# A state scan in halves or whole: merging the two half-row decays and scans of a Mamba block

## The chip, the cores and the metric

One core of one Trainium2 chip. The metric is the device time of one execution in microseconds (us). Times are written as the profile has them: us from the start of the span, durations in us unless marked ns. The five engines are PE (TensorE), DVE (VectorE), ACT (ScalarE), POOL (GpSimd) and SP (SyncE); PEld is the loading of weights into PE.

## The reference

The input is `x` of 8 sequences x 512 positions x 128 features, all fp32. Four layers follow one another, each of the form x = x + f(layernorm(x)): a Mamba block, a feed-forward block with ternary weights, a minimal GRU, and the same feed-forward block again. The change touches the Mamba block, whose core is a linear recurrence over the 512 positions, for 256 inner channels and 16 states:

```python
dA = jnp.exp(dt_s[..., None] * A)
hstate = dA * hstate + (dt_s * u_s)[..., None] * B_s[:, None, :]
y = jnp.einsum('bdn,bn->bd', hstate, C_s)
```

`dt` and `u` depend on sequence, position and channel, `A` on channel and state, `B` and `C` on sequence, position and state. The state starts at zero for every sequence.

## The kernel before, in words

The 256 channels lie as two halves (`HALVES`) of 128 partitions; positions run along the free dimension. So for one sequence b and one state n the whole recurrence is two rows of 512 elements per partition. The kernel walks over the 8 sequences and, inside, the 16 states: 128 steps, numbered g = 16 b + n. One step is:

- `mix_decay` (ACT, lines 700 and 702): dA = exp(dt * A), one ACTIVATE per half, into the PSUM tensor `dA` of 2 x 512 elements. There is a single `dA`, so a decay overwrites what the scan of the step before has read.
- `mix_inflow` (POOL, line 381; the very first on DVE): `inflow` = dtu * B, both halves in one instruction, in two buffers. It waits until the scan of step g - 2 is done.
- `mix_scan` (DVE, lines 922 and 925): `tensor_tensor_scan`, state = dA * previous + inflow along the 512 positions, one instruction per half, into one of three `state` buffers.
- `mix_cn` (PE, line 1197): a matmul that spreads C over the partitions into the PSUM tensor `c_ps`; it waits for the read of the step before.
- `mix_read` (DVE, line 933): state = state * C, both halves in one instruction.
- `mix_acc` (PE, line 1206): eight 128x128 transposes that add the result to `y_ps`.

The halves are chained by their own semaphores: the decay of half 0 waits for the scan of half 0 of the step before (`s_scan0`), the decay of half 1 for that of half 1 (`s_scan`); the scan of half 0 waits for the decay of half 0 (`s_dA0`), that of half 1 for the decay of half 1 (`s_dA`).

Everything else, that is all four layers of the earlier and later sequences, is woven between these steps. Each operation has a due time in steps, from tables written out at the top (`POOL_AT`, `ACT_AT`, `DVE_AT`, `PE_AT`, with exceptions for the first and the last sequence in `MOVED`), and every engine emits its operations in the order of these times, in quarter steps. Each engine then runs its queue strictly in order and waits on semaphores. The decay of step g is due at g - 1, the scan at g, the read at g + 0.75. Between them stand on ACT the normalisations (`n_tok`, L716, `n_hi`, L723), GELU and its table loads (L735), the GRU's inputs (L748, L753) and gates (L766); on DVE the GRU's products and scans (L1018, L1024), `in_hi` (L1009), `n_lo` (L985), statistics (L955 to L964) and residual sums (L948, L1002, L1031); on POOL `in_lo` (L536), roots and sums. PE's other products share three PSUM banks, `work`, in an order fixed when the program is built. SP issues all DMAs.

Of the kernel before, what the change touches and what calls it, by code (L numbers as in the profile page):

```python
# [12 lines left out]
ALU = mybir.AluOpType  # L13
ACT = mybir.ActivationFunctionType
# [3 lines left out]
ROWS, SEQ, D = 8, 512, 128  # L18
# [3 lines left out]
STATE = 16  # L22
# [159 lines left out]
def build(nc, x, gamma, beta, W_in, W_conv, b_conv, W_x, W_dt, b_dt, A_log, Dskip, W_out,  # L182
          W1, b1, W2, b2, Wz, bz, Wh, bh, Wo, bo, w_up, w_down, out):
    ctx = ExitStack()
    with ctx:
        def sb(name, shape, dt=F32):
            return ctx.enter_context(nc.sbuf_tensor(name, shape, dt))

        def sem(name):
            return ctx.enter_context(nc.semaphore(name))  # L190

        def flat(a):
            return a.rearrange("p a b -> p (a b)")
# [3 lines left out]
        ones = sb("ones", [P, P])  # L197
# [9 lines left out]
        decay_c = sb("decay_c", [P, HALVES, STATE])  # L207
# [27 lines left out]
        dt = sb("dt", [P, 2, HALVES, SEQ])  # L235
# [3 lines left out]
        inflow = sb("inflow", [P, 2, HALVES, SEQ])  # L239
        state = sb("state", [P, 3, HALVES, SEQ])  # L240
# [11 lines left out]
        scale = {m: sb("scale%d" % m, [P, TILES]) for m in NORMS}  # L252
# [28 lines left out]
        def pb(name, shape):  # L281
            return ctx.enter_context(nc.psum_tensor(name, shape, F32))

        dA = pb("dA", [P, HALVES, SEQ])
# [22 lines left out]
        s_conv, s_u, s_ztok = sem("conv_added"), sem("u_ready"), sem("z_tok_ready")  # L307
        s_xdhi, s_brow = sem("xd_hi_ready"), sem("b_row_ready")
        s_sparg, s_spexp, s_spln = sem("softplus_args"), sem("softplus_exp"), sem("softplus_ln")
        s_dt, s_dtu = sem("dt_ready"), sem("dtu_ready")  # L310
        s_bstored, s_bring = sem("b_stored"), [sem("b_ring%d" % k) for k in range(RING)]
        s_y0, s_cps = sem("y_started"), sem("c_full")
        s_dA0, s_scan0 = sem("decay_half_ready"), sem("scan_half_done")
        s_dA, s_inflow, s_scan, s_read, s_acc = (sem("decay_ready"), sem("inflow_ready"), sem("scan_done"),
                                                 sem("read_ready"), sem("acc_done"))
        s_gtok = sem("gated_tok_ready")
# [13 lines left out]
        def wait(eng, s, value):  # L330

            if value > 0:
                eng.wait_ge(s, value)
# [258 lines left out]
        def _(act):  # L592
# [102 lines left out]
            def mix_decay(b, n):  # L695

                if n == 0:
                    act.wait_ge(s_dt, HALVES * b + HALVES)
                wait(act, s_scan0, STATE * b + n)
                act.activation(dA[:, 0, :], dt[:, b % 2, 0, :], ACT.Exp, scale=decay_c[:, 0, n:n + 1]).then_inc(s_dA0, 1)  # L700
                wait(act, s_scan, STATE * b + n)
                act.activation(dA[:, 1, :], dt[:, b % 2, 1, :], ACT.Exp, scale=decay_c[:, 1, n:n + 1]).then_inc(s_dA, 1)  # L702

            def mix_gated(b, h, r, s):
                p = "gt%d" % h
# [65 lines left out]
            for r, s in slots():  # L771
# [6 lines left out]
                for n in range(STATE):  # L778
                    for b in due(r, s, ACT_ON["decay"], n):
                        mix_decay(b, n)  # L780
# [46 lines left out]
        def _(dve):  # L827
            def prepare_mix():
                dve.wait_ge(s_w_mix, W_MIX)
                dve.tensor_copy(win_hi[:, :], win_f).then_inc(s_win_hi, 1)  # L830
                dve.tensor_copy(wdt_hi[:, :], wdt_f).then_inc(s_wdt_hi, 1)
                dve.wait_ge(s_win_hi, 1)
                dve.tensor_tensor(win_lo[:, :], win_f, win_hi[:, :].bitcast(F32), ALU.subtract).then_inc(s_win, 1)
                dve.wait_ge(s_wdt_hi, 1)
                dve.tensor_tensor(wdt_lo[:, :], wdt_f, wdt_hi[:, :].bitcast(F32), ALU.subtract).then_inc(s_wdt, 1)
                for h in range(HALVES):
                    last = dve.tensor_scalar(diag[:, h, :], ident[:, :], skip_c[:, h:h + 1], None, ALU.mult)
                last.then_inc(s_diag, 1)
                dve.wait_ge(s_expA, 1)
                dve.tensor_scalar(decay_c[:, :, :], decay_c[:, :, :], -1.0, None, ALU.mult).then_inc(s_A, 1)  # L840

            def ternary_sums():
                dve.wait_ge(s_w_tail, W_TAIL)
                dve.tensor_reduce(abs_sum[:, 0:1], up_raw, AX_X, ALU.add, apply_absolute_value=True
                                  ).then_inc(s_abs, 1)
                dve.tensor_reduce(abs_sum[:, 1:2], down_raw, AX_X, ALU.add, apply_absolute_value=True
                                  ).then_inc(s_abs, 1)
# [68 lines left out]

            def mix_scan(b, n):
                g = STATE * b + n
                dve.wait_ge(s_dA0, g + 1)
                dve.wait_ge(s_inflow, g + 1)  # L920
                wait(dve, s_acc, g - 2)
                dve.tensor_tensor_scan(state[:, g % 3, 0, :], dA[:, 0, :], inflow[:, n % 2, 0, :],  # L922
                                       0.0, ALU.mult, ALU.add).then_inc(s_scan0, 1)
                dve.wait_ge(s_dA, g + 1)
                dve.tensor_tensor_scan(state[:, g % 3, 1, :], dA[:, 1, :], inflow[:, n % 2, 1, :],  # L925
                                       0.0, ALU.mult, ALU.add).then_inc(s_scan, 1)

            def mix_read(b, n):
                g = STATE * b + n
                dve.wait_ge(s_scan0, g + 1)  # L930
                dve.wait_ge(s_scan, g + 1)
                dve.wait_ge(s_cps, g + 1)
                dve.tensor_tensor(state[:, g % 3, :, :], state[:, g % 3, :, :],  # L933
                                  c_ps[:, :].unsqueeze(1).broadcast_to([P, HALVES, SEQ]), ALU.mult
                                  ).then_inc(s_read, 1)
# [101 lines left out]
            for r, s in slots():  # L1037
# [8 lines left out]
                for n in range(STATE):  # L1046
                    for b in due(r, s, DVE_ON["scan"], n):
                        mix_scan(b, n)
                for n in range(STATE):
                    for b in due(r, s, DVE_ON["read"], n):  # L1050
                        mix_read(b, n)
                for b in due(r, s, DVE_ON["norm"]):
                    mix_norm(b)
                for b in due(r, s, DVE_ON["apply"]):
                    mix_apply(b)
                    if b == 0:
                        prepare_mix()
# [335 lines left out]
```

## Time and profile before

| | us |
|---|---|
| median of 3 runs | 888.83 (888.02 to 889.85) |
| the profiled execution, own time | 888.83 |
| its span | 887.0 |
| busy PE / PEld / DVE / ACT / POOL | 712.8 / 594.5 / 708.8 / 632.2 / 592.9 |

The profile is a record of one execution. Its page lists the busy time of each engine and the costliest groups of instructions, with the idle time of the engine just before them and what ended it. The granted clock of PE is given as a share of full speed. A start-to-start distance on one engine can be shorter than the first instruction's duration, as the end of one overlaps the beginning of the next. From some 42 to 771 us the 128 steps run; from about 306 to 683 us they repeat with a period of about 94.6 us for each sequence of 16 steps.

### The profile page before, as it was taken

Reading aid. Unit: us, or ns where it says so; the run is one execution under the profiler, and the core shown is the slowest. Engines: PE = TensorE matmul, PEld = TensorE weight load, DVE = VectorE, ACT = ScalarE, POOL = GpSimd, SP = SyncE. Lnnn points to the kernel's source line nnn. Section 1 sums busy time; section 2 is a strip of 40 time slices with the busy share of each in tenths; the row PEclk is TensorE's granted clock in tenths of the full one; section 3 lists DMA queues with packets and bytes.
Section 4 is the critical chain, followed back from the end, with each engine's and each line's share of the span. In section 5 each row is a group of like instructions: output and inputs, shape, how many; then the busy total and the mean of one; then the engine's idle time right before and its main releaser. Section 6 shows DMA issues by size and latency. Waiting matters only on the chain. (4 is left out here: it accounts for less than half of the span.)

```text
span 887.0 us, 12459 instructions
## 1 busy us (share of the span) xinstructions
PE 712.8 (80%) x4058; PEld 594.5 (67%) x4058; DVE 708.8 (80%) x1092; ACT 632.2 (71%) x944; POOL 592.9 (67%) x374
## 2 busy tenths in 40 slices
PE   2363665669969996899879986999699968997976
PEld 2253554648857785768767876788577857786765
DVE  2479887899988989799989997999899997843231
ACT  4764666778788968897798779897889477526322
POOL 3178956876796869686979687877958567615312
PEclk9555757889989999899989998999889988999995
DMA  2341112121111111121111211121111101000000
GB/s 46 109 165 52 61 60 56 40 61 49 48 48 50 60 36 57 42 60 53 56 50 37 71 48 48 43 68 41 44 49 60 50 34 38 13 1 1 13 1 13
DMA packets 35186, 42.80 MB, mean 48 GB/s; under 512 B 7457, under 2 KB 17074, under 8 KB 35122
## 3 DMA queue, kind: packets, MB, share of 16 engines
q1 hardware_dynamic: 35122, 42.00, 15.6%
q8 instruction: 33, 0.54, 0.3%
q14 instruction: 31, 0.25, 0.1%
HBM read 39.63 MB, written 2.36 MB: 47 GB/s over the span
## 5 line engine op out<-in xcount | busy, mean ns | idle before, releaser
L381 POOL TENSOR_TENSOR inflow<-dtu,b_all 128x1024 f32<-128x1024 f32 x127 | 311.8, 2458 | 123.8 <-DVE state L925 94.0
L1206 PE MATMUL y_ps<-ident,state 128*128 128x128 f32 x1024 | 154.1, 300 | 29.0 <-DVE state L933 29.0
L933 DVE TENSOR_TENSOR state<-state,c_ps 128x1024 f32<-128x1024 f32 x128 | 155.4, 1214 | 27.0 <-PE c_ps L1197 23.8
L1206 PEld LDWEIGHTS y_ps<-ident,state 128*128 128x128 f32 x1024 | 135.9, 157 | 45.9 <-DVE state L933 35.1
L922 DVE TENSOR_TENSOR_SCAN state<-dA,inflow 128x512 f32<-128x512 f32 x128 | 155.5, 1215 | 5.3 <-ACT dA L700 4.2
L925 DVE TENSOR_TENSOR_SCAN state<-dA,inflow 128x512 f32<-128x512 f32 x128 | 153.0, 1195 | 0.0
L700 ACT ACTIVATE dA<-dt,decay_c 128x512 f32<-128x512 f32 x128 | 88.0, 687 | 58.5 <-DVE state L922 52.9
L1113 PE MATMUL work<-in_hi,wzh_hi 128*128 128x512 f32 x256 | 105.8, 413 | 5.5 <-POOL in_lo L536 5.1
L1115 PE MATMUL work<-in_lo,wzh_hi 128*128 128x512 f32 x256 | 101.1, 395 | 0.0
L1114 PE MATMUL work<-in_hi,wzh_lo 128*128 128x512 f32 x256 | 100.8, 394 | 0.0
L702 ACT ACTIVATE dA<-dt,decay_c 128x512 f32<-128x512 f32 x128 | 87.3, 682 | 17.0 <-DVE state L925 16.4
L1197 PE MATMUL c_ps<-xd,pick 128*128 128x512 f32 x128 | 62.7, 490 | 25.4 <-DVE state L933 25.3
L527 POOL TENSOR_TENSOR wide<-wide 128x512 f32<-128x512 f32 x48 | 61.1, 1273 | 20.4 <-ACT wide L740 18.0
L1113 PEld LDWEIGHTS work<-in_hi,wzh_hi 128*128 128x128 f32 x256 | 48.2, 188 | 22.5 <-POOL in_lo L536 12.9
L520 POOL TENSOR_TENSOR root<-vv,plus_half 128x8 f32<-128x8 f32 x16 | 26.4, 1648 | 46.6 <-DVE vv L964 46.6
L1242 PE MATMUL work<-n_hi,up_t 128*128 128x512 f32 x64 | 34.7, 542 | 28.0 <-DVE n_lo L985 12.4
L1115 PEld LDWEIGHTS work<-in_lo,wzh_hi 128*128 128x128 f32 x256 | 48.1, 188 | 11.2
L1114 PEld LDWEIGHTS work<-in_hi,wzh_lo 128*128 128x128 f32 x256 | 48.3, 189 | 8.9
L536 POOL TENSOR_TENSOR in_lo<-wide,in_hi 128x512 fp32r<-128x512 f32 x32 | 43.2, 1370 | 15.9 <-DVE in_hi L1009 15.9
L1197 PEld LDWEIGHTS c_ps<-xd,pick 128*128 128x128 f32 x128 | 27.9, 218 | 38.6 <-DVE state L933 32.3
L1024 DVE TENSOR_TENSOR_SCAN mixed<-keep,mixed 128x512 f32<-128x512 f32 x32 | 50.8, 1606 | 0.0
L735 ACT ACT_TABLE_LOAD x27 | 34.6, 1283 | 19.8 <-PE work L1243 19.6
(163 smaller groups left out, 1570.9 us busy)
## 6 DMA issues: line engine op xcount, KB each, us to landing
b_all<-b_scratch SPq DMA_DIRECT2D x128, 256.0 KB, 3.1
x_tok<-in_x SPq DMA_DIRECT2D x8, 256.0 KB, 3.8
out_x<-x_tok SPq DMA_DIRECT2D x8, 256.0 KB, 3.6
wide<-in_Wz SPq DMA_DIRECT2D x1, 1024.0 KB, 7.1
wide<-in_Wh SPq DMA_DIRECT2D x1, 1024.0 KB, 9.4
skip_f<-in_W SPq DMA_DIRECT2D x2, 256.0 KB, 5.3
dtu<-in_W_in SPq DMA_DIRECT2D x1, 256.0 KB
b_scratch<-gated SPq DMA_DIRECT2D x8, 32.0 KB, 1.8
```

What stands on the lines that cost most here:

```text
L381: eng.tensor_tensor(inflow[:, n % 2, :, :], dtu[:, :, :], b_all[:, n % RING, :].unsqueeze(1).broadcast_to([P, HALVES, SEQ]), ALU.mult).the ...
L527: pool.tensor_tensor(square[:, 0, :], square[:, 0, :], square[:, k, :], ALU.add).then_inc(s_sqsum[c], 1)
L700: act.activation(dA[:, 0, :], dt[:, b % 2, 0, :], ACT.Exp, scale=decay_c[:, 0, n:n + 1]).then_inc(s_dA0, 1)
L702: act.activation(dA[:, 1, :], dt[:, b % 2, 1, :], ACT.Exp, scale=decay_c[:, 1, n:n + 1]).then_inc(s_dA, 1)
L922: dve.tensor_tensor_scan(state[:, g % 3, 0, :], dA[:, 0, :], inflow[:, n % 2, 0, :], 0.0, ALU.mult, ALU.add).then_inc(s_scan0, 1)
L925: dve.tensor_tensor_scan(state[:, g % 3, 1, :], dA[:, 1, :], inflow[:, n % 2, 1, :], 0.0, ALU.mult, ALU.add).then_inc(s_scan, 1)
L933: dve.tensor_tensor(state[:, g % 3, :, :], state[:, g % 3, :, :], c_ps[:, :].unsqueeze(1).broadcast_to([P, HALVES, SEQ]), ALU.mult).then_i ...
L1113: pe.matmul(dst, w_hi, r_hi, start=start, stop=False)
L1114: pe.matmul(dst, w_lo, r_hi, start=False, stop=False)
L1115: return pe.matmul(dst, w_hi, r_lo, start=False, stop=stop)
L1197: pe.matmul(c_ps[:, :], pick[:, n:n + 1].broadcast_to([P, P]), xd[:, b % 2, :], start=True, stop=True).then_inc(s_cps, 1)
L1206: last = pe.matmul(y_region(j, h), state[:, g % 3, h, cols(j)], ident[:, :], is_transpose=True, start=False, stop=(n == STATE - 1), skip_g ...
```

## The change

The two half scans become one scan over 1024 elements. For this the first element of the second half of `dA` is set to zero once, so that the running value is multiplied by zero where the second half begins; the second decay then writes only elements 1 to 511 of its half, and so the zero stays. Both decays wait for the whole scan of the step before, the scan waits for both decays, and the semaphores `s_dA0` and `s_scan0` go.

```diff
@@ mix_decay
                 if n == 0:
                     act.wait_ge(s_dt, HALVES * b + HALVES)
-                wait(act, s_scan0, STATE * b + n)
-                act.activation(dA[:, 0, :], dt[:, b % 2, 0, :], ACT.Exp, scale=decay_c[:, 0, n:n + 1]).then_inc(s_dA0, 1)
+                    act.wait_ge(s_zero, 1)
                 wait(act, s_scan, STATE * b + n)
-                act.activation(dA[:, 1, :], dt[:, b % 2, 1, :], ACT.Exp, scale=decay_c[:, 1, n:n + 1]).then_inc(s_dA, 1)
+                act.activation(dA[:, 0, :], dt[:, b % 2, 0, :], ACT.Exp, scale=decay_c[:, 0, n:n + 1])
+                act.activation(dA[:, 1, 1:SEQ], dt[:, b % 2, 1, 1:SEQ], ACT.Exp, scale=decay_c[:, 1, n:n + 1]
+                               ).then_inc(s_dA, 1)
@@ prepare_mix (once, before the first sequence)
                 dve.tensor_scalar(decay_c[:, :, :], decay_c[:, :, :], -1.0, None, ALU.mult).then_inc(s_A, 1)
+                dve.tensor_scalar(dA[:, 1, 0:1], ones[:, 0:1], 0.0, None, ALU.mult).then_inc(s_zero, 1)
@@ mix_scan
-                dve.wait_ge(s_dA0, g + 1)
+                dve.wait_ge(s_dA, g + 1)
                 dve.wait_ge(s_inflow, g + 1)
                 wait(dve, s_acc, g - 2)
-                dve.tensor_tensor_scan(state[:, g % 3, 0, :], dA[:, 0, :], inflow[:, n % 2, 0, :],
-                                       0.0, ALU.mult, ALU.add).then_inc(s_scan0, 1)
-                dve.wait_ge(s_dA, g + 1)
-                dve.tensor_tensor_scan(state[:, g % 3, 1, :], dA[:, 1, :], inflow[:, n % 2, 1, :],
+                dve.tensor_tensor_scan(flat(state[:, g % 3, :, :]), flat(dA[:, :, :]), flat(inflow[:, n % 2, :, :]),
                                        0.0, ALU.mult, ALU.add).then_inc(s_scan, 1)
@@ mix_read
-                dve.wait_ge(s_scan0, g + 1)
                 dve.wait_ge(s_scan, g + 1)
```

## Rows read from the trace of the kernel before

**Rows 1.** The page, part 1: busy time, share of the span, instructions.
```profile
PE 712.8 (80%) x4058; PEld 594.5 (67%) x4058; DVE 708.8 (80%) x1092; ACT 632.2 (71%) x944; POOL 592.9 (67%) x374
```

**Rows 2.** Stretch, length, busy PE, PEld, DVE, ACT, POOL (count), PE clock, DMA, GB/s.
```profile
42.00:145.00 103.00, 60.30 (x278) 49.77 (x278) 88.24 (x100) 61.40 (x89) 75.34 (x38) 0.65 0.25 81
306.00:683.00 377.00, 337.39 (x2027) 283.27 (x2026) 342.56 (x524) 317.22 (x471) 295.23 (x181) 0.96 0.17 51
```

**Rows 3.** Costliest groups: busy, mean ns | idle before, releaser.
```profile
L933 DVE TENSOR_TENSOR state<-state,c_ps 128x1024 f32<-128x1024 f32 x128 | 155.4, 1214 | 27.0 <-PE c_ps L1197 23.8
L922 DVE TENSOR_TENSOR_SCAN state<-dA,inflow 128x512 f32<-128x512 f32 x128 | 155.5, 1215 | 5.3 <-ACT dA L700 4.2
L925 DVE TENSOR_TENSOR_SCAN state<-dA,inflow 128x512 f32<-128x512 f32 x128 | 153.0, 1195 | 0.0
L700 ACT ACTIVATE dA<-dt,decay_c 128x512 f32<-128x512 f32 x128 | 88.0, 687 | 58.5 <-DVE state L922 52.9
L702 ACT ACTIVATE dA<-dt,decay_c 128x512 f32<-128x512 f32 x128 | 87.3, 682 | 17.0 <-DVE state L925 16.4
L1024 DVE TENSOR_TENSOR_SCAN mixed<-keep,mixed 128x512 f32<-128x512 f32 x32 | 50.8, 1606 | 0.0
```

**Rows 4.** Waits: engine and line <- releaser: us in total, times, longest.
```profile
ACT dA L700 <- DVE state L922: 52.9, 32, 5.7
ACT dA L702 <- DVE state L925: 16.4, 39, 0.4
```

**Rows 5.** Timeline of DVE, one undisturbed step: start, duration, instruction.
```profile
85.88 1.22 DVE L922 TENSOR_TENSOR_SCAN state<-dA,inflow 128x512 f32<-128x512 f32 x1
87.02 1.20 DVE L925 TENSOR_TENSOR_SCAN state<-dA,inflow 128x512 f32<-128x512 f32 x1
88.31 1.22 DVE L933 TENSOR_TENSOR state<-state,c_ps 128x1024 f32<-128x1024 f32 x1
```

**Rows 6.** Line L922 by itself: duration ns min/median/max.
```profile
L922 DVE TENSOR_TENSOR_SCAN state<-dA,inflow x128: 1208/1215/1226, 42.8 to 769.2; 128x512 f32<-128x512 f32 x128
```

**Rows 7.** Timeline of ACT, then DVE, around 575 us.
```profile
575.15 0.67 ACT L702 ACTIVATE dA<-dt,decay_c 128x512 f32<-128x512 f32 x1
...
575.25 1.22 DVE L922 TENSOR_TENSOR_SCAN state<-dA,inflow 128x512 f32<-128x512 f32 x1
```

**Rows 8.** Timeline around 505 to 517 us, ACT then DVE.
```profile
511.27 0.67 ACT L702 ACTIVATE dA<-dt,decay_c 128x512 f32<-128x512 f32 x1
...
505.66 0.69 DVE L948 TENSOR_TENSOR x_tok<-work,base_tok 128x512 f32<-128x512 f32 x1 [1.07 <-PE work L1224]
...
511.53 1.22 DVE L922 TENSOR_TENSOR_SCAN state<-dA,inflow 128x512 f32<-128x512 f32 x1
...
516.70 0.75 DVE L1018 SCALAR_TENSOR_TENSOR mixed<-work,bh_c,gate 128x512 f32<-128x512 f32 x1 [0.60 <-PE work L1115]
```

**Rows 9.** Timeline of PE, then ACT, 529 to 544 us.
```profile
529.87 0.47 PE L1242 MATMUL work<-n_hi,up_t 128*128 128x512 f32 x1 [2.00 <-DVE x_tok L1031]
...
543.74 1.28 ACT L735 ACT_TABLE_LOAD   x1 [1.73 <-PE work L1243]
```

**Rows 10.** Timeline of ACT, then PE, around 183 us; DVE's wait at 160.64.
```profile
182.83 0.69 ACT L702 ACTIVATE dA<-dt,decay_c 128x512 f32<-128x512 f32 x1 [0.42 <-DVE state L925]
...
185.25 0.47 PE L1234 MATMUL work<-ident,n_tok 128*128 128x128 f32 x1 [3.27 <-ACT n_tok L716]
...
160.64 1.22 DVE L922 TENSOR_TENSOR_SCAN state<-dA,inflow 128x512 f32<-128x512 f32 x1 [1.94 <-ACT dA L700]
```

**Rows 11.** The chain that ended last: start, us, what; then DVE at 762.
```profile
698.60 0.69 ACT dA L700
...
766.29 0.87 PE y_ps L1206 x8
...
762.09 1.22 DVE L922 TENSOR_TENSOR_SCAN state<-dA,inflow 128x512 f32<-128x512 f32 x1 [1.78 <-ACT dA L700]
```

**Rows 12.** Timeline of DVE before the first step.
```profile
38.75 1.29 DVE L907 SCALAR_TENSOR_TENSOR dt<-work,dt 128x512 f32<-128x512 f32 x2 [6.74 <-ACT dt L693]
```

More of the change, by code:

```diff
@@ L309, in build @@
         s_sparg, s_spexp, s_spln = sem("softplus_args"), sem("softplus_exp"), sem("softplus_ln")
-        s_dt, s_dtu = sem("dt_ready"), sem("dtu_ready")
+        s_dt, s_dtu, s_zero = sem("dt_ready"), sem("dtu_ready"), sem("zero_ready")
         s_bstored, s_bring = sem("b_stored"), [sem("b_ring%d" % k) for k in range(RING)]
         s_y0, s_cps = sem("y_started"), sem("c_full")
-        s_dA0, s_scan0 = sem("decay_half_ready"), sem("scan_half_done")
         s_dA, s_inflow, s_scan, s_read, s_acc = (sem("decay_ready"), sem("inflow_ready"), sem("scan_done"),
```

## The prediction

> **What bounds the kernel now.** I read the page first [rows 1]: PE is busy for 80% of the span, DVE for 80%, ACT for 71%, POOL for 67%. No engine is the bound by itself. The busy time by stretch [rows 2] separates four regimes. From 42 to 145 us (sequence 0, the first of eight) DVE is at 86% and PE at a granted clock of 0.65. From 306 to 683 us, four sequences of about 94.6 us each, DVE (91%) and PE (89%, clock 0.96) are both nearly full. From 771 us no scan is left and PE sets the pace. One steady sequence, 494.40 to 588.98, stands as the model of the middle. Then the costliest groups [rows 3]: the two half scans are 155.5 + 153.0 us of DVE, the two half decays 88.0 + 87.3 us of ACT, the read 155.4 us. Then who waits [rows 3, 4]: DVE has waited for a decay 4.2 us in all, while ACT has waited 32 times (52.9 us) for the first half scan and 39 times (16.4 us) for the second. So the decays mostly come early, and what the change touches is the distance by which they do.
>
> **The merged scan.** In a step where nothing interferes [rows 5] the first scan starts at 85.88, the second at 87.02 and ends at 88.22: 2.34 us from start to end, and over the 128 steps I take 2.33. The first scan's start-to-start is 1.13 to 1.14 us. The read, twice as many elements, has the same duration, 1.214 [rows 3]. If the two clock at one rate, the scan takes two cycles where the read takes one, so of 1.13 us some 1.067 grow with the 512 elements and 0.066 are fixed. One scan of 1024 is then 1.215 + 1.067 = 2.282 us long; the step's scan work shrinks by 2.331 - 2.282 = 0.049 us, and 128 of them by 6.3 us. No row shows one instruction over both halves of `dA`, which are two tensors' worth of 512 in PSUM. Bounds: below, the fixed part goes twice, 2.20 us (another 0.08 less, 10 us in all); above, nothing overlaps and a second start is paid inside, 2 x 1.215 = 2.43 us (+0.10 per step, +12.7 us in all). The scans of `keep` and `mixed` average 1.606 us [rows 3], but those read two tensors from SBUF; the scans over `dA` at L922 all stay within 1.208 to 1.226 whatever POOL does [rows 6], so that is no end. I take 2.282, nearest to the plain pair.
>
> The Trainium skill (Perfetto Trace Analysis, section Optimizing Scalar/DVE Operations) gives a fixed data-access cost per DVE instruction of about 60 ns on SBUF and 125 ns on PSUM; by it, as an estimate, 128 fewer instructions save 7.7 to 16 us where DVE is saturated. The pair's 0.066 us [rows 5] sits at the lower figure.
>
> **What the whole wait costs.** Now both halves of the next decay wait for the whole scan. After it ends: 0.03 us to the first decay, 0.62 to the second's start, 0.68 for it, 0.03 to the scan: the scan can start 1.36 us after the last ended. Before, it needed only the first decay. From the timelines I put this beside each of the 127 gaps. In 92 the next scan started later than that anyway. In 35 it did not, and these are of two kinds.
> - Ten short gaps of 1.22 us (one 1.29), holding only the read, where ACT was ready and waiting [rows 5]. Each lacks 1.36 - 1.22 = 0.14 us: 1.3 us in all. Against its 0.05 gain such a step loses 0.09.
> - 25 steps where ACT came late with other work and the scan ran beside the second decay. Per steady sequence there are four. At 575.25 [rows 7] the scan starts as the first decay ends, while the second ends at 575.82: 0.6 us. At 511.53 [rows 8] the second ends at 511.94: 0.46 us. The other two are 0.26 each. That is 1.6 us per steady sequence against 16 x 0.05 = 0.8 saved; over all 25 it is 10.4 us.
>
> Gross, then: -6.3 + 1.3 + 10.4 = +5.4 us if all of it were on the path.
>
> ACT also comes later: where it waited for the first half [rows 4], the pair now ends 0.62 us later. Over 58 steps that is 33 us of shifts, most in front of another ACT wait.
>
> **What of it is on the path.** In the steady sequence, going along it:
> - From 575 to the place of 516 us in the next sequence PE runs nearly without a gap. The 0.6 at 575.25 is gone by the place of 505.66, where DVE waits 1.07 us for PE [rows 8]. The 0.46 at 511.53 meets a 0.60 us wait for PE at 516.70. Cover: PE's own queue; if that cover were gone each costs its full size.
> - From 517 to 543 us DVE is saturated and PE waits for it (2.00 us for L1031) [rows 9]. Four merged scans gain 4 x 0.05 = 0.2 us. ACT's shifts there (0.6 us, twice) end in its 1.7 us wait for PE at 543.74 [rows 9].
> - From 543 to 575 the chain runs over PE, DVE and POOL; ACT's 0.3 us shift reaches the PE products of `in0` to `in7`, but POOL's `in_lo` is later.
> Sum: -0.2 us per sequence, five of them, -1.0 us.
>
> Sequence 0: stretches with only the read lose 0.09 where others gain 0.05, and where DVE waits for PE neither counts: 0. Sequence 1 has two places on the path: the scan at 160.64, which waited for the decay itself (+0.6), and the decays at 181.72 and 182.83 [rows 10]. There ACT waited for both halves, `n_tok` stands right behind, PE waited 3.27 us for it, and then n_hi and n_lo, back to back. +0.6 goes through; with DVE's savings I take +0.8 there. The last sequence: at 699.31 [rows 11] the chain that ended last goes decay, scan: +0.6. At 762.09 [rows 11] another +0.6; its read ends near 765.7 and PE uses it at 766.29 on the chain, so 0.3 gets through. Less 0.15 of savings: +0.7.
>
> **Queues.** ACT's waits are in order, so what stands behind the longer one is its other work of the slot (n_tok, gelu, silu): counted above. POOL's inflow waits for the whole scan as before, and gains the 0.05. PE waits for the read, not the scan. SP's loads wait for inflow: nothing moves. The column set to zero is one instruction on 128x1 before the first sequence, where DVE waits 6.74 us for ACT before 38.75 [rows 12]: zero, and between 0 and 0.2 us. One wait less on the read and one fewer increment per step: zero, as the read starts 0.08 us after the scan's end by data alone. 511 elements instead of 512: 1 ns.
>
> **The sum.** 0 + 0.8 - 1.0 + 0.7 = +0.5 us. The profiled execution took 888.83 us (span 887.0, 1.8 around it), the median also 888.83: 889.3 us. About 0.2%, or 1.8 us, is what a measurement can tell; this is no change.
>
> **Rivals.**
> - A, DVE pays for everything: DVE is at 91% in the steady stretch [rows 2], PE waits on it. If late decays are absorbed but each saving counts: -6.3 + 1.3 = -5.0, 883.8 us. Against: 505.66 and 516.70, where DVE itself waits. 0.19.
> - B, slower: the decay pair becomes the bound. Place: the 25 steps with a late ACT, above all 575.25, 699.31, 762.09. It decides wherever the second decay ends less than 0.03 us before the scan's old start and nothing later waits. All on the path: +5.4, 894.2 us. For: ACT is at 84% in the steady stretch [rows 2], and has its table loads in front of these decays. 0.28. The Trainium skill (the same page and section) says that breaking up instructions may let work complete sooner where ACT and DVE are not saturated but cause bubbles elsewhere; the change does the reverse, and by that rule B is the outcome.
> - C, the merged scan pays a second start (2.43 us): against the plain merge 0.15 us more per step, 19 us; half of it on the path on top of the forecast is 898.8 us. Against: the even 1.13 spacing. 0.07.
> - D, no fixed part is left in the scan (2.20 us): 10 us less than the plain merge; half of it on the path is 884.3, all of it on top of A 873.6 us. 0.04.
> - The forecast: 0.42.
>
> **Chances and range.** Faster is A and D: 0.23. Slower is B and C: 0.35. Within 0.2%: 0.42. The forecast's own range is 887.3 to 890.6. The range for 8 in 10 is 885.0 to 893.5: it takes in A partly paid for by PE waits and B without its last tenth.
>
> **What would show it.** Scan L922 gone to one instruction of 2.28 us x128; if 2.43 or 2.20, C or D. DVE waiting for ACT's decay some 30 times instead of a few, about 9 to 11 us in total; if under 5 us, A. ACT's wait for the scan: one line, about 55 to 70 us, some 58 times. The steady sequence still 94.4 to 94.6 us between the same scans; 95.4 would be B, 93.9 A. The forecast is wrong if the steady sequence moves by more than 0.4 us, or if the stretch from 771 us on, which holds no scan, changes its length.

## The result and the profile after

| | kernel before | the change |
|---|---|---|
| median | 888.84 us (888.02 to 889.85, 4 runs) | 896.61 us (894.42 to 897.43, 4 runs) |
| ratio, 95% interval | | 1.0085 [1.0068, 1.0102] |
| the profiled execution | 888.83 us | 889.54 us |

The change makes the kernel slower, by 0.6 to 0.9%. The forecast was 889.3 us, no change. A trap lies in the last line: the one profiled execution of the change, which is not among the four of its median, came out at 889.54, next to the forecast, while its other executions took 894 to 897. Two more measurements of the same program gave 1.0062 [1.0039, 1.0085] and 1.0060 [1.0012, 1.0107], with profiled executions of 898.61 and 896.77 us.

The page of the profile after, part 1, and its windows, with the columns of [rows 2]:

```profile
PE 710.7 (80%) x4058; PEld 592.8 (67%) x4058; DVE 704.4 (79%) x965; ACT 628.4 (71%) x944; POOL 593.0 (67%) x374
```
```profile
42.00:145.00 103.00, 56.74 (x282) 46.86 (x282) 91.52 (x83) 63.36 (x95) 75.57 (x39) 0.68 0.25 80
306.00:683.00 377.00, 336.68 (x2017) 283.11 (x2016) 337.45 (x459) 312.13 (x466) 293.04 (x180) 0.95 0.17 50
```

DVE has 4.4 us less work than in [rows 1] and the kernel is no faster for it: in the 377 us of the steady stretch PE issued 2017 instructions for 2027 in [rows 2]. The groups that answer to [rows 3], the waits that answer to [rows 4], and the scan's durations beside [rows 6] (min/median/max, ns):

```profile
L923 DVE TENSOR_TENSOR_SCAN state<-dA,inflow 128x1024 f32<-128x1024 f32 x128 | 292.4, 2285 | 18.7 <-ACT dA L701 16.1
...
L700 ACT ACTIVATE dA<-dt,decay_c 128x512 f32<-128x512 f32 x128 | 88.0, 688 | 94.5 <-DVE state L923 90.0
...
L701 ACT ACTIVATE dA<-dt,decay_c 128x511 f32<-128x511 f32 x128 | 86.2, 673 | 0.0
```
```profile
ACT dA L700 <- DVE state L923: 90.0, 52, 6.4
...
PE work L1231 <- ACT n_tok L716: 30.4, 14, 6.5
...
DVE state L923 <- ACT dA L701: 16.1, 18, 2.8
```
```profile
L923 DVE TENSOR_TENSOR_SCAN state<-dA,inflow x128: 2274/2283/2292, 43.9 to 770.7; 128x1024 f32<-128x1024 f32 x128
```

The scan is one instruction of 2.285 us, 0.046 less than the pair's 2.33. DVE waits for a decay 16.1 us instead of 4.2, ACT waits for the scan 90.0 us instead of 52.9 + 16.4.

Where the time went is seen when the span is cut at the starts of scans. "7 to 10" is the time from the scan of state 7 to that of state 10, summed over sequences 2 to 6, "12 to 14" likewise, "other" the rest of those five sequences. All in us, worked out from the timelines of DVE:

| profile | first scan | seq. 0, 1 | 7 to 10 | 12 to 14 | other | seq. 7 to its last scan | after that | span |
|---|---|---|---|---|---|---|---|---|
| before | 42.8 | 169.6 | 94.2 | 69.7 | 307.2 | 85.7 | 117.8 | 887.0 |
| before again | 43.6 | 170.8 | 94.2 | 69.8 | 307.2 | 85.7 | 117.9 | 889.1 |
| change | 43.9 | 166.8 | 94.1 | 73.3 | 305.9 | 86.7 | 117.0 | 887.7 |
| change again | 44.0 | 169.3 | 97.6 | 73.3 | 306.0 | 86.0 | 120.7 | 896.8 |
| change, third | 44.1 | 170.5 | 96.4 | 73.3 | 305.9 | 87.2 | 117.4 | 895.0 |

The mean of the three less the mean of the two is +5.1 us: 12 to 14 gives +3.5, other -1.3, 7 to 10 +1.9, sequence 7 +0.9; the first scan (+0.8), sequences 0 and 1 (-1.3) and the end (+0.5) differ as much between executions of one program. States 12 to 14 and "other" repeat to 0.1 us in both programs. States 7 to 10 repeat in the kernel before but not in the change. The profile of the change that landed on the forecast is the one with the shortest 7 to 10, the shortest sequences 0 and 1 and the shortest end. Without it the difference is +7.9 us: 12 to 14 +3.5, other -1.2, 7 to 10 +2.8, sequence 7 +0.9, first scan +0.8, sequences 0 and 1 -0.3, end +1.2.

**States 12 to 14** (+0.7 us in each steady sequence). ACT, then DVE, of the change in the model sequence, whose scan of state 12 starts at 566.93:

```profile
565.27 0.69 ACT L700 ACTIVATE dA<-dt,decay_c 128x512 f32<-128x512 f32 x1 [0.19 <-DVE state L923]
565.90 0.67 ACT L701 ACTIVATE dA<-dt,decay_c 128x511 f32<-128x511 f32 x1
566.59 1.28 ACT L748 ACT_TABLE_LOAD   x1
567.88 1.26 ACT L748 ACTIVATE wide<-work,b_c 128x512 f32<-128x512 f32 x2
...
574.29 1.28 ACT L801 ACT_TABLE_LOAD   x1
575.59 0.69 ACT L700 ACTIVATE dA<-dt,decay_c 128x512 f32<-128x512 f32 x1
576.22 0.67 ACT L701 ACTIVATE dA<-dt,decay_c 128x511 f32<-128x511 f32 x1
```
```profile
572.99 2.95 DVE L1006 CAST in_hi<-wide 128x512 fp32r<-128x512 f32 x2
576.92 2.29 DVE L923 TENSOR_TENSOR_SCAN state<-dA,inflow 128x1024 f32<-128x1024 f32 x1 [0.98 <-ACT dA L701]
```
PE of the change, and then the same places of the kernel before, whose scan of state 12 starts at 566.30 (ACT, PE, DVE):

```profile
568.71 0.47 PE L1110 MATMUL work<-n_hi,w_hi 128*128 128x512 f32 x1 [0.61 <-ACT wide L748]
...
576.43 0.47 PE L1110 MATMUL work<-in_hi,wzh_hi 128*128 128x512 f32 x1
```
```profile
566.64 0.69 ACT L748 ACTIVATE wide<-work,b_c 128x512 f32<-128x512 f32 x1
567.50 0.69 ACT L748 ACTIVATE wide<-work,b_c 128x512 f32<-128x512 f32 x1 [0.17 <-PE work L1115]
...
573.23 1.28 ACT L801 ACT_TABLE_LOAD   x1
...
575.37 0.48 PE L1113 MATMUL work<-in_hi,wzh_hi 128*128 128x512 f32 x1
...
572.32 2.95 DVE L1009 CAST in_hi<-wide 128x512 fp32r<-128x512 f32 x2
```

Before, ACT waited for PE from the second GRU input on. Now the decays of state 12 start after the whole scan of state 11, the first input comes 0.95 us after the start of the scan of state 12 instead of 0.34, PE waits 0.61 for it, and PE's first `in_hi` product comes 9.50 us after that scan instead of 9.07. The pair of state 13, behind this, ends 9.96 us after it, and the scan waits 0.98 where in [rows 7] it needed only the first decay and ran right behind the casts: step 12 to 13 is 9.99 us for 8.95, the next 4.66 for 5.00. Part of the rest comes back later: at the place of 505.66 [rows 8], reached 33.94 us after the scan of state 12 before and 34.19 after, 0.25 us is left.

**States 7 to 10.** Windows from the scan of state 7 to that of state 10 in sequence 4: before, the change (third), and the kernel of e15 below, which has nothing of the change. Columns as in [rows 2].

```profile
445.40:463.12 17.72, 14.43 (x73) 11.40 (x73) 13.89 (x27) 16.00 (x25) 12.23 (x8) 0.81 0.17 51
```
```profile
447.61:467.31 19.70, 16.07 (x73) 13.11 (x73) 13.71 (x24) 16.93 (x27) 12.68 (x8) 0.74 0.15 53
```
```profile
443.90:464.06 20.16, 16.70 (x73) 13.38 (x73) 13.90 (x28) 16.43 (x25) 12.25 (x8) 0.66 0.19 52
```
The same 73 matrix instructions take 14.4, 16.1 and 16.7 us busy, at a mean granted clock of 0.81, 0.74 and 0.66 of 2.4 GHz: parts run at 1.2 GHz. Two groups of each window show it (mean ns of one; the line numbers of the e15 kernel are larger): in the change the products with `down_t` are longer, in e15 both groups. In e15 DVE waits for what became longer, where before it waited nowhere for these products:

```profile
L1242 PE MATMUL work<-n_hi,up_t 128*128 128x512 f32 x4 | 2.3, 574 | 0.4 <-DVE n_lo L985 0.4
...
L1255 PE MATMUL work<-down_t,wide 128*128 128x128 f32 x16 | 1.9, 275 | 0.0
```
```profile
L1252 PE MATMUL work<-down_t,wide 128*128 128x128 f32 x16 | 2.5, 321 | 0.0
L1239 PE MATMUL work<-n_hi,up_t 128*128 128x512 f32 x4 | 2.3, 574 | 0.4 <-DVE n_lo L982 0.4
```
```profile
L1264 PE MATMUL work<-down_t,wide 128*128 128x128 f32 x16 | 2.9, 354 | 0.0
L1251 PE MATMUL work<-n_hi,up_t 128*128 128x512 f32 x4 | 2.8, 706 | 1.0 <-DVE n_lo L994 1.0
...
460.22 1.13 DVE L1011 SCALAR_TENSOR_TENSOR x_tok<-work,rscale_a,x_tok 128x128 f32<-128x128 f32 x4 [1.46 <-PE work L1264]
```

The mean clock of this window doesn't decide its length by itself; here it matters where in it the lower clock falls. In the first profile of the change this window, 443.70 to 462.87, has a mean of 0.82 and is still 1.45 us longer than before. Before, there were two stretches near 0.5 of some 3.4 us, in the change one of 6.4 us, and DVE then waits 1.58 us for the `down_t` products, a wait that the kernel before doesn't have there. PE had stood idle for 2.28 and 1.68 us before the two falls, and for 1.68 before the one of the change; there a pause of 2.48 us some 6 us earlier was followed by no fall. Windows of before, then window and wait of the change:

```profile
446.60:449.90 3.30, 2.94 (x13) 2.35 (x12) 3.21 (x5) 2.31 (x5) 3.30 (x3) 0.52 0.32 73
452.90:456.40 3.50, 3.50 (x14) 2.91 (x14) 1.06 (x2) 3.45 (x6) 2.47 (x2) 0.54 0.22 76
```
```profile
451.10:457.50 6.40, 6.40 (x27) 5.81 (x27) 3.82 (x5) 6.32 (x9) 2.55 (x3) 0.51 0.20 68
...
459.06 1.13 DVE L999 SCALAR_TENSOR_TENSOR x_tok<-work,rscale_a,x_tok 128x128 f32<-128x128 f32 x4 [1.58 <-PE work L1252]
```

### The profile page after: what moved, and what is told of

Read it like the earlier page. It is cut to its first block, busy times and chain, and to the rows that moved or that the text cites. A ratio compares the mean times of both kernels' runs of the same rounds, so it can differ in the third digit from the quotient of the medians.

```text
span 887.7 us, 12333 instructions
## 1 busy us (share of the span) xinstructions
PE 710.7 (80%) x4058; PEld 592.8 (67%) x4058; DVE 704.4 (79%) x965; ACT 628.4 (71%) x944; POOL 593.0 (67%) x374
## 3 DMA queue, kind: packets, MB, share of 16 engines
HBM read 39.63 MB, written 2.36 MB: 47 GB/s over the span
## 4 chain that ended last, share of the span: by engine, by line
PE 44%; DVE 24%; issue 12%; POOL 10%; ACT 9%; DMA 0%; DVEq 0%; ACTq 0%; POOLq 0%
DVE state L923 10%; PE work L1110 7%; PE work L1112 7%; PE work L1111 7%; PE y_ps L1203 5%; PE work L1252 4%; DVE state L930 3%; POOL inflow L380 3%; POOL in_lo L535 3%; PE y_ps L1186 2%; PE c_ps L1194 2%; PE work L1239 2%; POOL wide L526 2%; ACT dA L701 1%; PE work L1221 1%
## 5 line engine op out<-in xcount | busy, mean ns | idle before, releaser
L923 DVE TENSOR_TENSOR_SCAN state<-dA,inflow 128x1024 f32<-128x1024 f32 x128 | 292.4, 2285 | 18.7 <-ACT dA L701 16.1
L700 ACT ACTIVATE dA<-dt,decay_c 128x512 f32<-128x512 f32 x128 | 88.0, 688 | 94.5 <-DVE state L923 90.0
L701 ACT ACTIVATE dA<-dt,decay_c 128x511 f32<-128x511 f32 x128 | 86.2, 673 | 0.0
L543 POOL TENSOR_SCALAR keep<-gate 128x512 f32<-128x512 f32 x32 | 20.3, 636 | 40.9 <-ACT gate L769 22.7
L766 ACT ACTIVATE gate<-work,bzh_c 128x512 f32<-128x512 f32 x32 | 21.8, 681 | 34.3 <-PE work L1112 32.7
```

The lines of the kernel that those rows point to most:

```text
L701: act.activation(dA[:, 1, 1:SEQ], dt[:, b % 2, 1, 1:SEQ], ACT.Exp, scale=decay_c[:, 1, n:n + 1]).then_inc(s_dA, 1)
L923: dve.tensor_tensor_scan(flat(state[:, g % 3, :, :]), flat(dA[:, :, :]), flat(inflow[:, n % 2, :, :]), 0.0, ALU.mult, ALU.add).then_inc(s_ ...
```

## The experiments

Every run is the program with one edit, timed beside the kernel before. The medians of the kernel before lay at 889.3 to 891.5 us in these measurements, with executions from 886.1 to 894.5, so ratios are compared, not times.

**The change once more.** No edit.

> The changed kernel once more, nothing else. Its first runs were 889.5 and six of 894.4 to 897.4 us against 888.0 to 889.9 before. Theory W (waits: the longer waits cost about 8 us in most executions, by pushing the steady sequences of 16 steps to a longer period, and the profiled execution was one that escaped): median 894 to 898 us, at least one run in five or more under 891, and a profile of a slow execution shows the steady period at 95.4 us or more instead of 94.6, spread over all sequences. Rival S (start: the slow runs lose their time once, in the first 145 us, where DMA and PE's clock differ from run to run): the same median, but a slow profile has the old period of 94.6 us and a late first sequence.

896.57 us, 1.0062 [1.0039, 1.0085]. The loss is real. No execution came under 891 this time, and the profile has the steady period at 95.3 us over sequences 2 to 5, with sequences 0 and 1 as before (169.3 for 169.6).

**Two scans with whole waits**, that is the change without the merged instruction:

```diff
-                wait(act, s_scan0, STATE * b + n)
+                wait(act, s_scan, STATE * b + n)
@@ mix_scan
-                dve.wait_ge(s_dA0, g + 1)
+                dve.wait_ge(s_dA, g + 1)
```

> Two half scans as before, but both decays wait for the whole scan of the step before, and the first half scan waits for both decays: the waits of the change without the merged instruction. Theory W: as slow as the change plus the 0.05 us per step that the merged scan saves where DVE is the bound, 895 to 901 us. Rival M (the merged scan or the decay of 511 elements costs time itself): 888 to 890 us.

899.81 us, 1.0106 [1.0082, 1.0129]. The waits alone cost more than the change; merging gives back 3.2 us of medians (e2's fastest execution, 898.75, is above the slowest of the change, 898.61).

**The two waits apart.** e3 has the first replacement of that diff alone (the decays' wait), e4 the second alone (the scan's).

> Only the first decay's wait is changed: it waits for the whole scan of the step before. The first half scan starts with the first decay as before. Theory W1 (what costs is ACT coming 0.6 us later in 58 steps, and with it n_tok, GELU and the GRU inputs): most of the change's loss, 893 to 897 us. Theory W2 (what costs are the 25 scans that can't start beside the second decay): 888 to 890 us.

> Only the first half scan's wait is changed: it starts when both decays are done. The first decay still waits for the first half scan alone. Theory W2: the 25 late scans, 10.4 us gross, are most of the loss, 892 to 897 us. Theory W1: 888 to 891 us.

e3: 894.76 us, 1.0052 [1.0031, 1.0073]. e4: 891.33 us, 1.0003 [0.9984, 1.0022]. So the part that the prediction priced highest, the scan that waits for both decays (10.4 us gross), costs nothing by itself that can be measured, and the part that it let go almost free, ACT's later decays, costs some 4 us. But the two don't add to the whole: with the decays' wait in place, the scan's wait costs 5.1 us more (e2 against e3, same measurement). Half of the 1.06% is there only when both are; by the three intervals that half, 0.5%, is itself good to some 0.4% (an estimate).

**Half waits back at single states**, in the kernel of e2:

```diff
+HALVES_APART = (5, 6)        # e6: (11, 12); e7: all but 5, 6, 11, 12
-                wait(act, s_scan, STATE * b + n)
+                wait(act, s_scan0 if n in HALVES_APART else s_scan, STATE * b + n)
@@ mix_scan
-                dve.wait_ge(s_dA, g + 1)
+                dve.wait_ge(s_dA0 if n in HALVES_APART else s_dA, g + 1)
```

> The two half scans with whole waits (8.8 us slower than before, where the whole wait of the decays alone cost 3.7 and that of the scan alone 0.3), but the waits by halves are back at states 5 and 6 of each sequence. There, in the kernel before, ACT waited for the first half scan with GELU, its table loads and then n_tok of the last feed-forward block right behind, and PE waited 2.3 us for that n_tok. Theory P (one place: the shift of 0.6 us in ACT at states 5 and 6 reaches n_tok and so PE): recovers 5 us or more, 891 to 895 us against 889 to 891 for before. Rival E (evenly: each late decay costs a little wherever it is): recovers a sixth or so, 1 to 2 us, 897 to 899 us.

> The same with the waits by halves back at states 11 and 12 only, where n_tok and n_hi of the GRU's norm and the GRU's inputs stand behind the decays. Theory P: recovers 1 to 3 us, 896 to 898 us. Rival E: 1 to 2 us, as at 5 and 6. Rival Q (the GRU inputs, which alternate between PE and ACT, are the place): 5 us or more, 891 to 895 us.

> The waits by halves at all states but 5, 6, 11 and 12, which keep the whole waits. Theory P with Q: most of the loss stays, 5 us or more above before. Rival E: a quarter of the 8.8 us stays, 2 us above before.

1.0052 [1.0033, 1.0072], 1.0020 [1.0001, 1.0039], 1.0046 [1.0023, 1.0069]. Against e2's 1.0106 (another chip, so by ratios, each good to some 2 us) these recover 5, 8 and 5 us, 18 in all where there are only 9.4 to recover: the losses are no sum over places.

**Merged, except at four states.** Scans of states 4, 5, 6, 10, 11, 12 stay in halves, the decays of 5, 6, 11, 12 wait by halves, all else is the change.

```diff
+                if n in HALVES_APART or (n + 1) % STATE in HALVES_APART:
+                    (the two half scans of before)
+                else:
+                    (the merged scan of the change)
```

> The merged scan at ten of the sixteen states; half scans at states 4, 5, 6, 10, 11 and 12, and the decays of 5, 6, 11 and 12 wait by halves. If the place of the loss is at 5, 6, 11 and 12 and a merged scan saves what the pair of e1 and e2 shows (3.2 us for 128, so 2 us for 80): at or 1 to 2 us below before. Rival E: three quarters of the change's 5.5 us stay, 3 to 4 us above before.

> The kernel of e8_merged_but_at_four once more, on whichever chip this is. If its gain is real: 0.996 to 0.999 again. If it was the luck of one chip: 1.000 or above.

889.74 us, 0.9975 [0.9959, 0.9992], and on another chip 888.88 us, 0.9976 [0.9960, 0.9992]: faster than both kernels, twice. By its profiles the steady sequences are still 1.4 us longer than before (sequences 2 to 6: 472.4 both times, for 471.0); the gain is in sequences 0 and 1, 166.4 and 166.7 for 169.6 and 170.8. Sequence 1 is 86.9 us for 89.5, of which 1.9 in the step from state 1 to 2 (3.65 for 5.52). The change had that short step in one of its three profiles, and e3, e4 and e5 have it too, so the partial merge isn't what makes it; why it comes and goes stays open, and with it why this kernel is faster than the kernel before.

**ACT's square moved behind `n_tok`**, in the change (e9), in the kernel before (e10), and in a merged kernel with half waits at 11 and 12 only (e11):

```diff
-    "a.sum2": 21.5   "a.square2": 21.75   ("POOL", "a.sum3", 7): 22
+    "a.sum2": 22.25  "a.square2": 22.25   ("POOL", "a.sum3", 7): 22.25
```

> The change, with one ACT instruction of 0.62 us (the square a.square2, L740) moved from in front of the decay pair of state 7 to behind the n_tok of L716 that follows it, and the POOL sum that reads it (a.sum2, 1.27 us) moved to stand beside the next sum. In the change the decays of state 6 start 0.62 us later, ACT then runs without a gap up to n_tok, and PE waits for n_tok. The move gives n_tok its time back and leaves every wait of the change as it is. Theory N (the later n_tok, with the lower granted clock of PE's work behind it, is what states 5 to 10 lose): step 9 to 10 falls from 7.6 back towards 7.0 us, a steady sequence is 0.4 to 0.6 us shorter than the change's, and the time is 3 to 4 us less than the change's, a ratio of 1.002 to 1.004 to before. Theory S (the loss sits in the waits of DVE for its decays, not in n_tok): ratio 1.006 to 1.0085 as the change. Theory K (POOL, whose sum now stands in front of an inflow, takes it back): as the change or up to 1.01, with DVE waiting for an inflow at L923.

> The control: the same two moves made to the kernel before. There n_tok starts right after the decays with its offsets only just ready (offset at 537.37 to 537.55 us, n_tok at 537.71), so an earlier ACT has at most 0.15 us to give. Theory N: 0.999 to 1.001, the move is worth something only where the change made n_tok late. If the move by itself gains 3 us or more here (ratio under 0.997), a gain of the changed kernel with it says nothing on the change. Theory K: above 1.002.

> Merged scans except at states 10, 11, 12, whose scans stay in halves; the decays of 11 and 12 wait by halves; the decays of 5 and 6 wait for whole scans, and the square stands behind n_tok as in e9_change_square_behind. Theory N: the move does for states 5 and 6 what half waits did in e8_merged_but_at_four (0.9975), and one more pair of merged scans a sequence is worth 0 to 1 us: 0.996 to 0.999. If half waits at 5 and 6 do more than n_tok's time back: 1.000 to 1.003.

1.0101 [1.0078, 1.0124], 1.0048 [1.0030, 1.0066], 1.0062 [1.0040, 1.0085]. The control lost 0.5% by itself, so e9 and e11 say nothing on `n_tok`. All three lose 2.1 us in the step from state 6 to 7 in each of the sequences 2 to 5 (7.6 us for 5.5 in e10). DVE and POOL of e10:

```profile
540.38 2.36 DVE L879 TENSOR_SCALAR m_vv<-m_mv 128x4 f32<-128x4 f32 x1
...
540.37 2.34 POOL L381 TENSOR_TENSOR inflow<-dtu,b_all 128x1024 f32<-128x1024 f32 x1
```

With its sum moved away, POOL starts the inflow 0.01 us ahead of a 128x4 DVE instruction, which at this place takes 0.20 us in the kernel before and here as long as the inflow; the offsets, and `n_tok` with them, come 2 us late.

**A delay by itself**, in the kernel before: two ACT instructions on 128x80, 0.41 us together, once a sequence. (The rest of the edit declares `pad` and its semaphore and names the place.)

```diff
+                for k in range(2):
+                    act.activation(pad[:, k, :], ones[:, 0:80], ACT.Copy).then_inc(s_pad, 1)
```

> The kernel before, with nothing of the change, and two small idle ACT instructions (128x80 each, together some 0.5 to 0.7 us) in front of n_tok (L716) of the third norm, once a sequence, behind the decay pair of state 7. Theory N (a later n_tok is what costs in states 7 to 10): step 9 to 10 rises from 6.94 to some 7.5 us, the stretch around it shows more of the lower granted clock, a steady sequence is 0.4 to 0.9 us longer, ratio 1.003 to 1.006. Theory of the forecast (ACT's shift ends in its 1.7 us wait for PE): ratio 0.999 to 1.001 and step 9 to 10 unchanged.

> As e13_pad_ahead_of_n_tok, with the two instructions right behind n_tok, in front of the square, z_tok and n_hi. PE's products of n_tok come at their old time. Theory N in its narrow form (n_tok itself): 0.999 to 1.002. If n_hi and the decays behind it carry the loss, as much as e13: 1.003 to 1.006. Theory of the forecast: 0.999 to 1.001.

> The kernel before with the two idle ACT instructions once a sequence behind the decay pair of state 12, in front of the table load for the GRU's inputs (in0, L748). Theory T (the delay passes through ACT to the decays of state 13): step 12 to 13 rises from 8.95 to 9.4 to 9.6 us, of which up to 0.3 come back at once; a steady sequence 0.1 to 0.5 us longer, ratio 1.001 to 1.005. Theory of the forecast (PE's queue hides it): 0.999 to 1.001.

> The kernel before with the delays of e13 and of e15 together. If the losses add: the sum of what e13 and e15 cost. If they overlap, as e5 to e7 suggest: no more than the larger of them plus 1 us. If these two places are what the decays' longer wait costs, the ratio is that of e3_decays_wait_whole, 1.004 to 1.007.

0.9992 [0.9974, 1.0010], 1.0032 [1.0014, 1.0049], 1.0040 [1.0016, 1.0065], 0.9997 [0.9982, 1.0011]. A later `n_tok` alone didn't make the kernel slower, so theory N fails at this dose: `n_tok` starts 4.92 us after the scan of state 6 instead of 4.59, while the change puts it at 5.15. In its profile the step from state 9 to 10 does grow in four of the five sequences, by 0.2 to 0.6 us, as the theory has it, and falls by 1.4 in the fifth. The same delay behind `n_tok` costs 2.8 us. A delay at the inputs costs 3.6 us, and the same delay with a second one added costs nothing. Cut as above, sequences 2 to 6:

| profile | 7 to 10 | 12 to 14 | other | sum |
|---|---|---|---|---|
| before | 94.2 | 69.7 | 307.2 | 471.0 |
| e2 waits only | 96.8 | 73.8 | 306.4 | 477.0 |
| e3 decays' wait | 95.2 | 71.9 | 305.9 | 473.1 |
| e4 scan's wait | 94.7 | 71.6 | 305.9 | 472.3 |
| e13 ahead of n_tok | 94.8 | 69.6 | 305.9 | 470.2 |
| e14 behind n_tok | 97.2 | 69.7 | 305.8 | 472.6 |
| e15 ahead of in0 | 97.2 | 70.5 | 305.0 | 472.6 |
| e16 both | 93.8 | 70.5 | 305.0 | 469.3 |

These are single executions, and e3's was its fastest (890.92, with a median of 894.76), so 7 to 10 is to be read with care.

At 12 to 14 costs add: e3 +2.2, e4 +1.9, e2 +4.1; e15 +0.8, e16 +0.8. The step from state 12 to 13 shows the same: 8.95 us before, 9.38 in e3, 9.55 in e4, 9.99 in e2 and in the change. The -1.3 of "other" isn't a gain of the merge, as e13 and e14 have it with nothing merged; what it comes from stays open. At 7 to 10 costs don't add: a delay placed at state 12 moves it by +3.0, together with another by -0.4. In sequence 4 the two kernels take 20.16 and 17.96 us there, at mean clocks of 0.66 and 0.81. But PE's busy time alone doesn't give the sum over the sequences: it is 73.7 us before, 74.6 in e2 (+0.9, with the stretch +2.6) and 77.0 in e10 (+3.3, with the stretch +0.5). That where the lower clock falls is what moves this stretch is seen in the windows above; that it explains all of it isn't shown.

**Both programs once more**, for profiles.

> The kernel before, unchanged, for a second profile. If the stretches of a program differ between executions by where the granted clock falls: sequences 2 to 6 within 1.5 us of 471.0, the first two within 3 us of 169.6, the end (from the last scan's start) 117 to 121 us. If the steady sequences are what the change moves, sequences 2 to 6 stay under 473. If they come out at 474 or more, the change's +2.3 and +5.8 us there are an execution's own and prove nothing.

> The change, unchanged, for a third profile. If the loss is in the steady sequences: sequences 2 to 6 between 473 and 477.5 (471.0 before). If it is in the end: 120 us or more from the last scan's start, with sequences 2 to 6 near 471.

889.92 us, 0.9997 [0.9972, 1.0022], and 896.46 us, 1.0060 [1.0012, 1.0107]. Sequences 2 to 6: 471.1 and 475.6, with before at 471.0: the longer sequences are the change's and not one execution's.

## Why the prediction was wrong

Right:
- The scan's size: 2.285 us measured, 2.282 forecast; C and D fall. 128 x 0.046 is 5.9 us of DVE. By the fixed costs that the Trainium skill gives (Perfetto Trace Analysis, section Optimizing Scalar/DVE Operations) it would have been, as an estimate, 7.7 to 16: the trace lies below both. In sequences 2 to 6 the merge by itself, e2 against the change outside 7 to 10, gives 1.0 us, the -1.0 of the sum.
- The last sequence, in the mean: +0.7 forecast, +1.0, +0.3 and +1.5 measured. The scan at 762.09 [rows 11] now waits 2.42 us for 1.78.

Right in part:
- The late scans. Taken alone, they are hidden, as the prediction said of [rows 7] and [rows 8] (e4; and in the change the wait for PE at 516.70 went from 0.60 to 0.19 us as the scan in front of it came later). With ACT's decays late as well they are not: +5.1 us of medians, e2 over e3.
- Sequence 1. At 160.64 [rows 10] the step is 6.36 us for 5.59, and 0.44 comes back in the next; PE's wait for `n_tok` grew from 3.27 to 3.83. Yet other steps gained more, and the sequence is 89.2, 88.4 and 89.8 us for 89.6, where +0.8 was forecast.
- What would show it. DVE waits 16.1 us for decays, 18 times, where 9 to 11 us and some 30 times were forecast. ACT waits 90.0 us for the scan, 52 times, where 55 to 70 were forecast: that sum lacked the 1.14 us by which the end of the whole scan lies behind that of its first half, 32 times (52.9 + 36.5 = 89.4).

Wrong is the step on the steady sequences ("-0.2 us per sequence, five of them"), forecast -1.0 us, measured +2.3, +5.8 and +4.6. It put ACT's later decays at nothing, and they cost 0.52% by themselves (e3); and it priced each cover alone, while late decays and late scans together cost twice the sum of the two (e2: 1.06%, e3 and e4: 0.52 and 0.03). Two of its sentences fail in the traces.
- "ACT's 0.3 us shift reaches the PE products of `in0` to `in7`, but POOL's `in_lo` is later". The shift is 0.61, the whole of what the decay pair is late, as nothing on ACT absorbs it: its waits for PE there were 0.17 to 0.27 us. PE waits 0.61 for the input, and its `in_hi` products start 0.43 later (e3 has the same 9.50 us, e4 the old 9.07). There PE's unbroken run begins, which the prediction held to be a cover. What delays its start is not all hidden: 12 to 14 and "other" together are +0.46 us a sequence, 2.3 us over five. That the late start of the run is what carries this is argued. e15 started it 0.16 us later, and of that nothing was left at the place of 505.66 (33.78 us after the scan of state 12, for 33.94).
- The 33 us of ACT's shifts were set aside as "most in front of another ACT wait". It wasn't worked out place by place: in the change `n_tok` starts 0.56 us later (5.15 us for 4.59 after the scan of state 6). And the forecast took every PE duration as fixed. Between 7 and 10 they are not, and the stretch came out at 0, +3.4 and +2.3 us in the three profiles.

Rival B had the right sign, and its 894.2 us is nearer to the measured 896.6, with half of the mechanism: it put the 25 late scans on the path, and by themselves they aren't (e4). The Trainium skill's rule that was cited there (the same page and section), that breaking up instructions may let work complete sooner, agrees in its sign: the change, which joins two instructions, is slower. Its condition, engines that aren't saturated, fits ACT (84% in [rows 2]) better than DVE (91%). The test named in the prediction, a steady sequence 0.4 us longer, was met: 94.9, 95.3 and 95.0 us over sequences 2 to 5, for 94.1. The other, a changed end, was met in one profile: 120.7 us after the last scan's start, for 117.8.

The two profiles near the medians hold the whole loss: their spans are 7.9 us longer in the mean, against 5.5 to 7.8 us of medians. Of this, 12 to 14 with "other" (+2.3) repeats in every profile; the +2.8 of 7 to 10 and the +1.2 of the end vary between executions. That the clock in 7 to 10 alone accounts for the spread of executions is argued, not shown.

## What to carry to other kernels

Where a chained pair is merged, price the later start of the producer, ACT here, by following its queue to the next place where another engine waits for it. Then price the waits together and not one by one: here two that cost 0.52% and 0.03% apart cost 1.06% together. It can pay to merge by place and keep the halves where the producer comes late: that kernel, at 0.9975, lost 1.4 us in the steady sequences where the change lost 2.3 to 5.8, though what made it faster than the kernel before stays open. And one profile whose time agrees with the forecast proves nothing: look at the other executions, and cut two or three profiles into stretches to see which of them repeat.

## What the hardware showed that was not expected

- A scan of 1024 elements over both halves of `dA` in PSUM takes 2274 to 2292 ns, in all 128 cases: no second start inside.
- A DVE instruction on 128x4 took 2.36 us (e10) instead of 0.20 (before) beside a POOL instruction on 128x1024 that had started 0.01 us before it (the kernel before has 1.47 and 2.38 us for two such instructions in sequence 0); `dA` scans beside POOL never grew [rows 6].
- The same 73 matrix instructions took 14.4 to 16.7 us in one program place, at mean granted clocks of 0.81 to 0.66, and one execution each of e15 and e16, which differ by 0.41 us of ACT work a sequence placed elsewhere, took 20.16 and 17.96 us for the stretch around them.
